# Moving three down products of one batch into the next batch's softmax-to-feed-forward chain

## The reference

```python
q = qdq(ln(x)) @ qdq(wq).T + bq                    # 16 heads of 32
k, v = split(ctx @ wkv.T + bkv)
o = softmax(q @ k.T / sqrt(32)) @ v
x = x + tanh(g_x) * (qdq(o) @ qdq(wp).T + bp)
h = ln(x)
fuse = silu((h @ w8(gate_w)) * gate_scale) * ((h @ w8(up_w)) * up_scale)      # 1536 wide
out = x + tanh(g_f) * ((fuse @ w8(down_w)) * down_scale)
```

## Time and profile before

| | |
|---|---|
| median of 3 runs | 951.47 us |
| profiled execution, its own time | 953.38 us |
| its span, first to last instruction | 951.6 us |
| outside the span | 1.8 us |
| busy in the span: PE, DVE, ACT, POOL | 868.7, 672.6, 554.1, 259.4 us |
| mean granted TensorE clock | 0.978 of 2.4 GHz |
| batch 2 feed-forward | 702.1 to 778.25 us |
| batch 3 attention | 778.25 to 849.6 us |
| batch 3 chain | 849.6 to 885.4 us |
| batch 3 feed-forward and stores | 885.4 us to the end |

### The profile page before, as it was taken

How to read it: one execution, slowest core, us unless ns; L and a number is a source line. 1 busy time by engine, 2 the same in 40 slices (tenths; PEclk the granted TensorE clock), 3 DMA queues, 4 the chain that set the end, 5 groups by cost and what they waited for, 6 DMA issues and landing times.

```text
span 951.6 us, 13564 instructions
## 1 busy us (share of the span) xinstructions
PE 868.7 (91%) x4992; PEld 312.3 (33%) x5000; DVE 672.6 (71%) x1292; ACT 554.1 (58%) x693; POOL 259.4 (27%) x236
## 2 busy tenths in 40 slices
PE   5987898999899998999899998999899999983998
PEld 2421121135333331224443331224443332221443
DVE  6787968838666778868676779868767668676222
ACT  5546877652566566882556557883456559871330
POOL 1145889760037503000017603000003204000130
PEclk9998999999999998999999999999999999995999
DMA  9235244310201332200111133200100023200001
GB/s 335 87 86 137 73 124 121 120 43 0 50 23 45 95 112 50 52 1 1 39 34 46 43 119 95 51 1 1 33 18 2 15 81 92 55 1 0 1 1 44
DMA packets 37106, 55.28 MB, mean 58 GB/s; under 512 B 8944, under 2 KB 15152, under 8 KB 37040
## 3 DMA queue, kind: packets, MB, share of 16 engines
q1 hardware_dynamic: 35120, 48.13, 17.7%
q0 software_dynamic: 1920, 6.29, 2.3%
HBM read 31.21 MB, written 4.19 MB: 37 GB/s over the span
## 4 chain that ended last, share of the span: by engine, by line
PE 68%; DVE 13%; ACT 12%; issue 6%; DMA 1%; POOL 0%; ACTq 0%; DVEq 0%
PE ps L1274 33%; PE ps L1601 9%; PE ps L1416 9%; PE ps L1433 8%; ACT r L797 7%; PE ps L1395 4%; PE ps L1447 2%; DVE acc L1041 2%; PE ps L1455 1%; PE ps L1258 1%; DVE r L1173 1%; DVE am L896 1%; DVE r L1016 1%; ACT r L822 1%; ACT r L705 1%
## 5 line engine op out<-in xcount | busy, mean ns | idle before, releaser
L797 ACT ACTIVATE r<-ps 128x1024 f32<-128x1024 f32 x256 | 251.3, 1022 | 78.7 <-PE ps L1416 76.2
L1416 PE MATMUL ps<-qst,kst 97*128 97x512 f16 x512 | 141.5, 389 | 14.2 <-ACT r L797 12.9
L1016 DVE CUSTOM_DVE_ANT_0 kst<-ps,kst 128x512 f32<-128x512 f32 x192 | 124.5, 685 | 34.5 <-PE ps L1395 32.7
L1433 PE MATMUL ps<-r,vv 128*32 128x512 f32 x1024 | 138.1, 612 | 3.4 <-ACT r L797 3.2
L1041 DVE TENSOR_TENSOR acc<-acc,r 128x1024 f32<-128x1024 f32 x108 | 129.7, 1257 | 3.9 <-ACT r L797 3.5
L756 ACT ACTIVATE kst<-ps 128x1024 f32<-128x1024 f32 x96 | 98.2, 1023 | 56.4 <-PE ps L1330 56.1
L605 POOL TENSOR_TENSOR rstd<-mv,mhalf 128x4 f32<-128x4 f32 x8 | 9.9, 1239 | 347.4 <-DVE mv L927 347.4
L672 POOL TENSOR_TENSOR r<-xq,r 128x512 f16<-128x512 f32 x48 | 57.2, 1192 | 144.2 <-ACT r L847 143.7
L1274 PE MATMUL ps<-xs,w_gate 128*128 128x512 f16 x384 | 90.9, 380 | 1.5 <-DVE xs L1205 1.5
L1274 PE MATMUL ps<-xs,w_up 128*128 128x512 f16 x384 | 91.1, 380 | 0.0
L1416 PEld LDWEIGHTS ps<-qst,kst 97*128 97x128 f16 x512 | 37.6, 98 | 157.3 <-ACT r L797 110.5
(11 more groups left out here) (148 smaller groups left out, 1292.5 us busy)
## 6 DMA issues: line engine op xcount, KB each, us to landing
kst<-k_reg SPq DMA_DIRECT2D x192, 64.0 KB
qst<-q_reg SPq DMA_DIRECT2D x192, 32.0 KB
xs<-in_x SPq DMA_DIRECT2D x4, 1024.0 KB, 6.0
cf<-in_ctxT POOLq DMA_DIRECT2D x16, 256.0 KB, 3.5
xres<-in_x SPq DMA_DIRECT2D x4, 1024.0 KB, 5.3
out<-xres SPq DMA_DIRECT2D x16, 256.0 KB, 2.1
acc<-in_down_w SPq DMA_DIRECT2D x10, 256.0 KB, 2.6
vv<-in_wkvT SPq DMA_DIRECT2D x2, 1024.0 KB, 9.8
```

The lines of the kernel that those rows point to most:

```text
L797: nc.scalar.activation(prob[:, s:s + 2, :], ps[:, first_bank:first_bank + 2, :], ACT.Exp, scale=SCALE).then_inc(exp_done, 1)
L1016: ins = nc.vector.tensor_tensor_reduce(kept(b, n)[:, k, :], bank(PAIR + k), kept(b, n)[:, k, :], 1.0, -3.0e38, ALU.add, ALU.max, mx[:, g % ...
L1416: mm = nc.tensor.matmul(bank(first_bank + k), kst[0:97, g % 2, j + k, t * P:(t + 1) * P], qst[0:97, g % 2, j + k, :], start=True, stop=True)
L1433: mm = nc.tensor.matmul(ps[j * DH:(j + 1) * DH, O_BANK, :], vv[:, t, h * DH:(h + 1) * DH], prob[:, p_slot(b, u, j), :], start=(t == 0), st ...
```

## The change

DOWN1 to DOWN3 of batch 2 leave its feed-forward stage. They stand in batch 3's chain as LATE1 to LATE3: LATE1 and 16 matmuls of LATE2 after O3, the other 8 of LATE2 and all of LATE3 after PROJ3. DVE treats their tiles (`down_tile`) after the rounding of the attention output (LATE1), after the moments (LATE2) and after the normalisation (LATE3).

Since `r1` is full of exponentials then, the gated products of batch 2 go to `ctx_hi`, `ctx_lo` and `wkv_hi` (`f2_at`); since `xres` still holds batch 2's tiles, the residual of batch 3 goes to `wkv_lo` (`x_last`). SP stores tile 0 of batch 2 behind the keys of group 1 and the residual's load, and tiles 1 to 3 with batch 3's. The 34 slots of batch 2 stand at K2 to K7 (as before), after all 24 gate and up products, and four in DOWN0. The steps of batches 0 and 1 keep their order.

```diff
-DOWN_AT = {"DOWN0": (2, 6, 10), "DOWN1": (2, 6, 10), "DOWN2": (2, 6), "DOWN3": (1, 8)}
+DOWN_AT_LATE = {"DOWN0": (1, 4, 7, 10)}
+LATE = range(1, NT)
+AHEAD = [beside_products([k for k in range(2 * FT) if k % 4 != 3], DOWN_AT)] * (B - 2)
+AHEAD += [beside_products(range(2 * FT), DOWN_AT_LATE), {}]
...
+CHAIN_LATE = (CHAIN_LAST[0:5] + ["LATE1"] + CHAIN_LAST[5:13] + ["LATE2", "LATE3"] + CHAIN_LAST[13:])
+LATE_EARLY = 8
+D_SEQ = [CHAIN + HI_SEQ + ffn_seq(b) for b in range(B - 1)] + [CHAIN_LATE + ffn_seq(B - 1)]
...
+        x_last = wkv_lo[:, :, :].rearrange("p c n -> p (c n)").bitcast(F32).rearrange("p (t n) -> p t n", t=NT)
...
+        def f2_at(b, part, i):
+            if b != B - 2:
+                return f2[:, part, i, :]
+            k, n = divmod(part * FT + i, 2 * CT)
+            return (ctx_hi, ctx_lo, wkv_hi)[k][:, n // 2, n % 2 * N:(n % 2 + 1) * N]
+        def residual(b, t):
+            return x_last[:, t, :] if b == B - 1 else xres[:, t, :]
...
+                elif b == B - 2:
+                    sp.wait_ge(d_full, d_full_count(b, "K7"))
+                    load_residual(b + 1)
+                    store_rows(b, range(1))
+                else:
+                    store_rows(b - 1, LATE)
+                    store_rows(b, range(NT))
...
+            def down_tile(b, t, at, name):
+                dve.wait_ge(d_full, d_full_count(at, name))
+                if t >= 2:
+                    dve.wait_ge(x_done, b * NT + t - 1)
+                nc.vector.tensor_tensor(down[:, t % 2, :], bank(d_bank(at, name)), ds_bc[:, :],
+                                        ALU.mult).then_inc(d_free, 1)
+                dve.wait_ge(d_free, d_free_count(at, name))
+                nc.vector.tensor_tensor(residual(b, t), residual(b, t), down[:, t % 2, :], ALU.add).then_inc(x_done, 1)
...
+                    if kind == "LATE":
+                        for i in range(LATE_EARLY if n == 2 else 0, FT):
+                            mm = down_step(b - 1, out, n, i)
+                        mm.then_inc(d_full, 1)
+                        if n == 1:
+                            bank_free(b, "LATE2")
+                            for i in range(LATE_EARLY):
+                                down_step(b - 1, bank(d_bank(b, "LATE2")), 2, i)
...
-                    pe.wait_ge(d_free, max(d_free_count(b - 1, n) for n in FFN_SEQ if n[0] in "TD"
-                                           and d_bank(b - 1, n) in (first_bank, first_bank + 1)))
+                    for k in range(2):
+                        released(b - 1, [n for n in d_seq(b - 1) if d_bank(b - 1, n) == first_bank + k][-1])
```

More of the change, by code:

```diff
@@ L96 @@
 DOWN_AT = {"DOWN0": (2, 6, 10), "DOWN1": (2, 6, 10), "DOWN2": (2, 6), "DOWN3": (1, 8)}
[L97 to L106, removed]
@@ L109, with beside_products @@
[L109 to L115, removed]
+DOWN_AT_LATE = {"DOWN0": (1, 4, 7, 10)}
+def beside_products(gates, downs):
+    places = [f"K{n}" for n in range(2, 8)] + [f"GU{k}" for k in gates] + [n for n in downs for _ in downs[n]]
+    assert len(places) == len(DIFFS) + 2
+    steps = {}
+    for n, name in enumerate(places):
+        steps.setdefault(name, []).append(slot(n) if n <= len(DIFFS) else [("S", G - 1, 0)])
+    return steps
@@ L500, in shift_row, with store_rows @@
                 sp.dma_start(qst[96:97, g % 2, :, :], crow_rows(g)).then_inc(stack_in[g % 2], 16)
+            def store_rows(b, tiles):
+                rows = out[b].rearrange("(t p) c -> p t c", p=P)
+                for t in tiles:
+                    sp.wait_ge(x_done, b * NT + t + 1)
+                    sp.dma_start(rows[:, t, :], residual(b, t)).then_inc(stored, 16)
             def load_x(b):
@@ L1181, in _ @@
                 next_v(1, 2, 3)
+                if last:
+                    down_tile(b - 1, 1, b, "LATE1")
                 dve.wait_ge(x_biased, b * NT + NT)
@@ L1194, in _ @@
                     dve.wait_ge(d_free, d_free_count(b, name))
-                    x1_steps.append(step.mark(nc.vector.tensor_tensor(xres[:, t, :], xres[:, t, :], tmp[:, t % 2, :],
+                    x1_steps.append(step.mark(nc.vector.tensor_tensor(residual(b, t), residual(b, t), tmp[:, t % 2, :],
                                                                       ALU.add)))
-                whole(moments(xres, after=x1_steps))
+                whole(moments(x_last if last else xres, after=x1_steps))
                 next_v(5, 6)
+                if last:
+                    down_tile(b - 1, 2, b, "LATE2")
                 dve.wait_ge(rstd_ready, variance_of_x2(b))
-                for ins in normalised(x2, xres):
+                for ins in normalised(x2, x_last if last else xres):
                     ins.then_inc(x2_ready, 1)
+                if last:
+                    down_tile(b - 1, 3, b, "LATE3")
                 next_v(7)
@@ L1208, in beside @@
                 def beside(name):
-                    for part in AHEAD.get(name, []) if not last else []:
+                    for part in AHEAD[b].get(name, []):
                         maxima(b + 1, part)
@@ L1336, in bank_free, with released @@
                 before = d_before(b, name)
-                if before is None:
-                    pass
-                elif before[:2] == "GU":
+                if before is not None:
+                    released(b, before)
+            def released(b, before):
+                if before[:2] == "GU":
                     pe.wait_ge(fu_ready, b * FT + int(before[2:]) // 2 + 1)
@@ L1449, in sums, with down_step @@
                 mm.then_inc(p_used, 1)
+            def down_step(b, out, t, i):
+                for part in range(2):
+                    mm = nc.tensor.matmul(out, f2_at(b, part, i)[:, t * P:(t + 1) * P], w_down[:, i, :],
+                                          start=(i == 0 and part == 0), stop=(i == FT - 1 and part == 1))
+                return mm
             def totals(b, g):
@@ L1593, in _ @@
                         for i in range(FT):
-                            if ahead and i in DOWN_AT[name]:
+                            if ahead and i in (DOWN_AT_LATE if b == B - 2 else DOWN_AT)[name]:
                                 ahead.pop(0)()
@@ L1599, in _ @@
                                 pe.wait_ge(f_ready, b * FT + i + 1)
-                            for s in range(2):
-                                mm = nc.tensor.matmul(out, f2[:, s, i, n * P:(n + 1) * P], w_down[:, i, :],
-                                                      start=(i == 0 and s == 0), stop=(i == FT - 1 and s == 1))
+                            mm = down_step(b, out, n, i)
                         mm.then_inc(d_full, 1)
```

71 lines of the change are left out of this document (38 added, 33 removed).

## The result

| | before | changed |
|---|---|---|
| median | 951.43 us (951.26 to 953.22, 4 runs) | 938.0 us (936.7 to 938.6, 4 runs) |
| profiled execution, its own time | 953.38 | 936.7 |
| its span | 951.6 | 934.9 |
| mean granted TensorE clock | 0.978 | 0.991 |

The account below looks back on a forecast made before the run. PE was taken to bound batch 2's feed-forward while standing idle in batch 3's chain. Gains of 13.1 and 1.4 us sum to 14.5, taking the median from 951.47 to 937.0 us, range 934.4 to 940.4.

Parts of the forecast that it names:

- 72 matmuls, 15.6 us: Batch 2's feed-forward: three down products removed, 72 matmuls of 0.216 us, 15.6 us less before batch 3's first scores.
- Waits of the crowded slots: Batch 2's feed-forward: PE waits 0.3 us among products and 1.6 in DOWN0; vanished old waits return about 0.3.
- The bank, 0.9: Batch 3's first scores wait 0.9 us until DVE has read DOWN0 from bank 0.
- Attention, 0: Batch 3's attention keeps its length: the keys land with 5 us to spare, cost none.
- rival 3: Batch 3's attention: POOL's four residual additions slip between DVE's, each costing 1.0 us; 941.0 us, chance 0.08.
- Copies and projection, -1.3: Batch 3's chain: at full clock, copies, projection and DVE's first tile come 0.2, 0.4 and 0.7 us sooner.
- LATE2's tile, +0.6: Batch 3's chain, before the normalisation: DVE's tile costs 0.2 us, plus 0.4 for its addition waiting on POOL's power.
- X2T's clock, -0.6: X2T transposes, batch 3's chain: half clock as before or full, 1.3 us less; 0.6 taken.
- Sum: Whole kernel: 13.1 us before batch 3's first exponential plus 1.4 in its chain, 14.5 us less.
- Rival 1: Batch 2's feed-forward: DVE or ACT cannot follow the slots, waits add 3 us; 940.0 us, chance 0.14.
- Rival 2: Clock stays full through X2T, DVE's tile fits beside POOL, DOWN0's waits are half as long; 934.8 us, chance 0.13.
- Rival 4: Batch 3's chain: the clock falls before the moved products run, 15.4 us more; 953.8 us, chance 0.03.

Follow-up runs that it names:

- the two kernels that differ by the move alone: The changed kernel, and it with all down products back in batch 2, its new buffer places and crowded slots kept: 954.52 us, ratio 1.0029.
- the two-product kernel: The changed kernel with only two down products moved, DOWN1 staying in batch 2: 945.69 us, ratio 0.9943 to the kernel before.
- the one with all three edits: Changed kernel with 8 early LATE2 matmuls, DOWN0's and TOP3's banks swapped, DOWN0's slots at steps 3, 6, 9, 11: 938.81 us, ratio 0.9847.

## Why the prediction was right

- **72 matmuls, 15.6 us.** Right: the two kernels that differ by the move alone show 14.54, and 15.54 with the bank's wait of 1.00 between the starts added.
- **Waits of the crowded slots, 0.3 + 1.6, less 0.3 of old ones.** Measured 1.94 for 1.6. The 1.20 in DOWN0 came as worked out, and so did TOP3's wait (it starts 0.48 us behind the matmul ahead of it in place of 0.22: 0.26 for 0.3). What was too small is the term for the slots between the products: before the slot of 746.81 stands a wait of 0.30 where I took 0.1.
- **The bank, 0.9.** Measured 0.83 as idle time in the trace, 1.00 between the starts, and 0.88 by exchange of the banks.
- **Attention, 0.** Right in length. But the argument that DVE would not be disturbed was weak: the two-product kernel shows rival 3's mechanism at its price. The prediction gave it 0.08; the change escapes it because POOL is held, for a reason that no run shows. That part was luck.
- **Copies and projection, -1.3.** Measured -1.05, as the stretch to DVE's first tile is 3.76 instead of 3.5 us. DVE's tiles then gained 0.25 for 0.1.
- **LATE2's tile, +0.6.** This term was mis-sized: it cost 0.11. The 0.4 for POOL's power was taken from an addition of 128x512 on POOL; beside a power of 128x4 there was no hold. The tile's addition and the power overlapped, where the prediction had named it as a sign that they would not.
- **X2T's clock, -0.6.** Measured -0.43; the clock fell inside X2T. With the idle time filled it was -1.2. The prediction left open whether the clock would be at half and took the middle; the other traces of the same chain show -0.24, and -0.86 with 1.7 us lost behind it in the tail. So the closeness of this term, and the tail's 0, are luck. No term stood for a half clock in the gate products.
- **Sum.** -12.6 - 1.6 = -14.2 us in the changed stages, for -14.5. That it is so close owes something to luck as well: LATE2's tile came 0.5 us better than forecast, and the stage 0.5 us worse. The median came out 1.0 us above the forecast, which is less than the 2.46 us by which the two traces differ in their unchanged part.

Rival 1 is refuted (PE waits about 0.4 us in batch 2's gate and up products, not 3). Rival 2 fails on the clock and on DOWN0's waits; its third part, that DVE's tile fits beside POOL, came true. Rival 4 fails on the first rows of LATE, which lie 0.216 us apart at a clock of 1.00.

## What to carry to other kernels

A product taken from where PE sets the end is worth its full time, if it stands where PE waited anyway, and here it also kept the clock up there. Before such a move, look which bank the first operation behind it needs, and count the other engine's sum in the shortened tail. Then look at what the shift slides against what: a load that keeps its time while the attention starts earlier or later meets DVE at another point.

## What the runs showed of the hardware

One order of instructions does not fix where the clock falls. With 2.56 us of idle time before X2T and 1.49 behind it, the half clock held, in three traces, from 0.5 us after X2T's start until X2T was through, from before its start until just before its end, and from within X2T to the end of the first gate product. The two kernels with 4 steps of LATE2 ahead of OQT, both with 1.68 us of idle time there, had it at the projection in one trace and in the first gate products in the other. Only with 0.18 us of idle time before X2T (1.97 or 0.90 behind it) it stood nowhere from OQT on, in three traces of three kernels. Where it falls costs differently: 0.8 to 1.0 us in X2T, 1.7 where PE is busy throughout.

The spread between runs has to do with the clock too. Batch 1's attention and chain up to the projection, in which nothing was changed, in the kernel before and in the one with all three edits:

```profile
344.79:441.53 96.74, 90.86 (x559) 26.29 (x559) 77.48 (x100) 73.46 (x87) 9.09 (x5) 0.96 0.17 44
```

```profile
344.55:438.34 93.79, 87.98 (x558) 25.99 (x558) 77.32 (x100) 73.47 (x87) 9.10 (x5) 1.00 0.17 46
```

The work of DVE and ACT is the same; the clock is 0.96 and 1.00, and 2.95 us lie between them. In the changed kernel it was 95.17 us, which is 1.57 of the 2.46 us that its profiled run gained ahead of the change. Why the clock is lower in one execution than in another no run shows.
